# Expert up weights kept in SBUF and copied by the vector engine, in place of one load from HBM per block

## The reference, cut to what matters

```python
def _L1_ffn_ref(hidden_states, gate_w, e_bias, up_w, down_w, shared_up_w, shared_down_w):
    x = hidden_states.reshape(-1, H)                       # 2048 x 256
    topk_idx, topk_w = _router(x, gate_w, e_bias)          # 6 of 32 experts per token
    combine = jnp.zeros((T, N_EXPERTS)).at[jnp.arange(T)[:, None], topk_idx].add(topk_w)
    h = _relu2(jnp.einsum('th,eih->tei', x, up_w))         # 128 hidden units per expert
    h = h * combine[:, :, None]
    moe_out = jnp.einsum('tei,ehi->th', h, down_w)
    shared = _relu2(x @ shared_up_w.T) @ shared_down_w.T
    return (moe_out + shared).reshape(B, S, H)
```

## Time and profile before

| what | value |
|---|---|
| median of 3 runs | 829.08 us (828.86 to 834.64) |
| the profiled execution's own time | 829.08 us |
| its span | 827.3 us |
| PE busy over the span | 718.7 us (87%) |
| DVE / ACT / POOL busy | 392.1 / 276.7 / 309.9 us |
| DMA moved | 190.57 MB, mean 230 GB/s |
| mean granted TensorE clock | 0.939 of full speed |
| chain that ended last | PE 48%, POOL 17%, DVE 12%, DMA 10%, issue 9% |

### The profile page before, as it was taken

How to read it: one execution, slowest core, us unless ns; L and a number is a source line. 1 busy time by engine, 2 the same in 40 slices (tenths; PEclk the granted TensorE clock), 3 DMA queues, 4 the chain that set the end, 5 groups by cost and what they waited for, 6 DMA issues and landing times.

```text
span 827.3 us, 14657 instructions
## 1 busy us (share of the span) xinstructions
PE 718.7 (87%) x4703; PEld 633.6 (77%) x4703; DVE 392.1 (47%) x1508; ACT 276.7 (33%) x625; POOL 309.9 (37%) x328
## 2 busy tenths in 40 slices
PE   3898999989999999999999975898782799968766
PEld 3777788989999999999989953666561799957654
DVE  5999875223223223233223358788610344436453
ACT  2644532211111111111111123443330477745540
POOL 1333413730111011011010100777777277777670
PEclk9998877999999999999999986999996799989997
DMA  8999998358676676677673233555343899999996
GB/s 255 397 276 226 226 225 218 110 185 284 212 242 215 209 242 214 209 236 224 210 225 117 83 124 96 192 166 164 132 166 119 264 356 349 351 337 395 398 313 252
DMA packets 109945, 190.57 MB, mean 230 GB/s; under 512 B 11681, under 2 KB 75766, under 8 KB 109726
## 3 DMA queue, kind: packets, MB, share of 16 engines
q1 hardware_dynamic: 94464, 148.05, 58.4%
q0 software_dynamic: 13344, 38.68, 12.3%
q10 hardware_dynamic: 2046, 2.71, 1.1%
HBM read 143.44 MB, written 65.62 MB: 253 GB/s over the span
## 4 chain that ended last, share of the span: by engine, by line
PE 48%; POOL 17%; DVE 12%; DMA 10%; issue 9%; SPq 3%; ACT 1%; POOLq 0%; DVEq 0%; ACTq 0%
PE PB L598 21%; PE PB L623 12%; POOL rows_in L1880 11%; DMA MEM<-in_w 4%; POOL sorted_x L1846 4%; PE PB L814 3%; PE PB L825 3%; POOL rows_out L1892 2%; DMA X<-in_x 2%; PE PB L800 1%; PE PB L526 1%; DMA MEM<-rows_out 1%; DVE WK L1279 1%; DMA rows_out<-WS,MEM 1%; SPq L2093 1%
## 5 line engine op out<-in xcount | busy, mean ns | idle before, releaser
L598 PE MATMUL PB<-XT,MEM 128*128 128x128 f32 x1584 | 183.0, 275 | 0.6 <-DMA MEM<-in_w 0.4
L598 PEld LDWEIGHTS PB<-XT,MEM 128*128 128x128 f32 x1584 | 179.7, 192 | 1.1 <-DMA MEM<-in_w 0.6
L1855 POOL DMA_INDIRECT sorted_y<-WK x36 | 34.6, 962 | 260.1 <-DVE WK L1466 260.1
L1880 POOL DMA_INDIRECT rows_in<-MEM x96 | 94.0, 979 | 77.4 <-DVE MEM L1664 48.7
L623 PE MATMUL PB<-MEM,WK 128*128 x432 | 99.2, 379 | 0.0
L623 PEld LDWEIGHTS PB<-MEM,WK 128*128 128x128 f32 x432 | 79.3, 190 | 9.3
L814 PE MATMUL PB<-MEM 128*128 128x128 f32 x456 | 63.4, 284 | 17.6 <-DMA MEM<-in_w 17.6
L932 ACT ACTIVATE XT<-PB 128x256 f32<-128x256 f32 x52 | 20.0, 384 | 168.8 <-PE PB L580 168.8
L814 PEld LDWEIGHTS PB<-MEM 128*128 128x128 f32 x456 | 57.6, 198 | 20.2 <-issue 10.8
L1892 POOL DMA_INDIRECT rows_out<-WS,MEM x58 | 57.5, 992 | 33.6 <-ACT WS L1071 17.5
L1443 DVE TENSOR_TENSOR WK<-WK,PB 64x128 f32<-64x128 f32 x36 | 10.5, 292 | 114.4 <-ACT WK L942 114.4
(11 more groups left out here) (259 smaller groups left out, 1204.3 us busy)
## 6 DMA issues: line engine op xcount, KB each, us to landing
MEM<-in_w SPq DMA_DIRECT2D x36, 896.0 KB, 7.1
rows_in<-in_consts SPq DMA_DIRECT2D x32, 600.0 KB, 14.1
MEM<-in_w SPq DMA_DIRECT2D x148, 128.0 KB, 2.3
MEM<-in_w SPq DMA_DIRECT2D x36, 512.0 KB, 4.1
MEM<-rows_in SPq DMA_DIRECT2D x58, 300.0 KB, 4.9
MEM<-rows_out SPq DMA_DIRECT2D x16, 768.0 KB, 7.2
MEM<-in_w SPq DMA_DIRECT2D x2, 3072.0 KB, 19.4
sorted_x<-MEM SPq DMA_DIRECT2D x1, 5070.0 KB, 39.4
```

The source lines that it names most:

```text
L598: t = e.matmul(o[:, to:to + P], UPW[m][i % (3 - m)][:, k, c * P:(c + 1) * P], XT[:, n % 2, k, :], start=(k == 0), stop=(k == 1))
L1855: e.indirect_dma_start(out=DY, out_offset=bass.IndirectOffsetOnAxis(ap=DEST[:, i:i + 1], axis=0), in_=YS[:, i % 2, :], in_offset=None).the ...
L1880: e.indirect_dma_start(out=DX1, out_offset=bass.IndirectOffsetOnAxis(ap=SLOT1[:, i, j:j + 1], axis=0), in_=XR[:, i, :], in_offset=None).th ...
```

## The change

SP no longer loads up weights in the last stage. `load_expert` now loads both halves of an expert (256 KB instead of 128 KB, 32 times), so that `W1E` holds up and down weights of all experts. DVE reads the table of experts and copies the up weights of each block, 128 x 256 numbers, from `W1E` to a small buffer `WUP` (two pairs deep), at an address that comes from a register. PE's `up2` waits for that copy ("bw"). DVE makes the copies of pair s+1 right behind the multiplication of pair s, ahead of `sum_rows`; the reading of the table and `meta1` stand ahead of the multiplication.

```diff
-        W1E = MEM[:, 0:E1 * 256].rearrange("p (e c) -> p e c", e=E1)
-        W1U = MEM[:, 9216:11264].rearrange("p (a b c) -> p a b c", a=4, b=2)
+        W1E = MEM[:, 0:E1 * 512].rearrange("p (e c) -> p e c", e=E1)
+        WUP = WK[:, 3116:4140].rearrange("p (a b c) -> p a b c", a=2, b=2)
...
             def up2(s):
                 q.wait_ge("bxt", s)
-                q.wait_ge(f"wu{s % 4}", s)
+                q.wait_ge("bw", s)
...
-                        t = e.matmul(PB[:, 4 + s % 4, j * P:(j + 1) * P], W1U[:, s % 4, j, k * P:(k + 1) * P],
+                        t = e.matmul(PB[:, 4 + s % 4, j * P:(j + 1) * P], WUP[:, s % 2, j, k * P:(k + 1) * P],
                                      XTB[:, s % 3, j, k, :], start=(k == 0), stop=(k == 1))
...
+            def weights2(s):
+                q.wait_ge("bu", s - 2)
+                for j in range(2):
+                    t = e.tensor_copy(WUP[:, s % 2, j, :], W1E[:, bass.ds(expert(packed, 2 * s + j), 1), 0:256].rearrange(
+                        "p e c -> p (e c)"))
+                t.then_inc(*q.mark("bw", s))
+
...
             def step(s, n_pairs):
                 if s + 1 < n_pairs and (s + 1) % 2 == 0:
+                    q.wait_ge("tabe")
+                    if s < 0:
+                        for j in range(4):
+                            q.wait_ge(f"w1{j}", 8 * j + 7)
+                    packed[(s + 1) // 2] = four_experts(q, (s + 1) // 2)
+                    if s < 0:
+                        weights2(0)
                     meta1((s + 1) // 2)
                 if 0 <= s < n_pairs:
                     ht = HT1[:, s % 3, :, :].rearrange("p b c -> p (b c)")
                     q.wait_ge("brl", s)
                     e.tensor_tensor(ht, ht, PB[:, 4 + s % 4, 0:256], ALU.mult).then_inc(*q.mark("bh", s))
+                if 0 < s + 1 < n_pairs:
+                    weights2(s + 1)
...
-                    e.dma_start(W1E[:, k, :], w1[SC + k, :, 256:512]).then_inc(*q.land(f"w1{k // 8}", k))
+                    e.dma_start(W1E[:, k, :], w1[SC + k]).then_inc(*q.land(f"w1{k // 8}", k))
...
-            def weights2(s):
-                q.wait_ge("tabe")
-                if s // 2 not in packed:
-                    packed[s // 2] = four_experts(q, s // 2)
-                q.wait_ge("bu", s - 4)
-                for j in range(2):
-                    e.dma_start(W1U[:, s % 4, j, :],
-                                w1[bass.ds(expert(packed, 2 * s + j) + SC, 1), :, 0:256].rearrange("e p c -> p (e c)")
-                                ).then_inc(*q.land(f"wu{s % 4}", *((s,) if j else (s, "first"))))
```

More of the change, by code:

```diff
@@ L95 @@
     "cleared": ("set", "hb0"),
[L96 to L99, removed]
 }.items() for signal in list_}
@@ L823, in down2 @@
                 for j in range(2):
-                    w = W1E[:, bass.ds(expert(packed, 2 * s + j), 1), :].rearrange("p e c -> p (e c)")
+                    w = W1E[:, bass.ds(expert(packed, 2 * s + j), 1), 256:512].rearrange("p e c -> p (e c)")
                     t = e.matmul(PB[:, 2 + s % 2, j * D:(j + 1) * D], HT1[:, s % 3, j, :], w, start=True, stop=True)
@@ L1747, in dve_program @@
             number1 = e.value_load(PAGES, min_val=0, max_val=P)
+            packed = {}
             def meta1(k):
@@ L2083, in store @@
                 e.dma_start(od[:, i:i + 2, :], X[:, i:i + 2, :]).then_inc(*q.land("out_a", i))
-            packed = {}
-            def weights2(s):
-                q.wait_ge("tabe")
-                if s // 2 not in packed:
-                    packed[s // 2] = four_experts(q, s // 2)
-                q.wait_ge("bu", s - 4)
-                for j in range(2):
-                    e.dma_start(W1U[:, s % 4, j, :],
-                                w1[bass.ds(expert(packed, 2 * s + j) + SC, 1), :, 0:256].rearrange("e p c -> p (e c)")
-                                ).then_inc(*q.land(f"wu{s % 4}", *((s,) if j else (s, "first"))))
-            for s in range(3):
-                weights2(s)
             fetched = 6
@@ L2103, in step @@
             def step(s, n_pairs, fetched):
-                if 3 <= s + 3 < n_pairs:
-                    weights2(s + 3)
                 for k in range(fetched, min(s + 8, n_pairs + n_pairs % 2)):
@@ L2121, in end1 @@
                 n_pairs, k = PAIRS[c], fetched
-                packed.clear()
                 for s in range(COMMON, n_pairs + 2):
```

## The result

| | before | changed |
|---|---|---|
| median of 19 runs each | 834.64 us | 841.01 us |
| lowest and highest | 828.86, 838.26 us | 837.46, 846.13 us |
| profiled execution, span | 829.08, 827.3 us | 839.12, 837.3 us |

The ratio is 1.0077, with a 95% interval of 1.0056 to 1.0097: the changed kernel is slower by about 6.4 us. The forecast was 838.5 us, and the range (825 to 862) holds the time. The profiled execution of before was at the low end of its 19 runs, so the two profiles are 10.0 us apart, the two medians 6.4 us.

The account below looks back on a forecast made before the run. POOL was taken to bound the last stage, with 7 us to spare. Last up2 12.7 us later, tail 3.8 us shorter, larger loads 0.5 us: 9.4 us on the profiled 829.08, so 838.5 us, range 825 to 862.

Parts of the forecast that it names:

- the ring: Last stage: up2, relu, square, two copies, next up2 wait on each other in turn; 2.72 us a pair, against POOL's 2.54.
- Part 1: Last stage: 114 loads of 128 KB go, and PE's 17.6 us of waits; gains at most POOL's spare 7 us.
- Part 2: Between the layers: 32 loads grow by 128 KB each, 4.2 MB in all; costs 0.5 us.
- Part 3: Last stage's new loop: up2 waits for copies behind the previous square, so the bound leaves POOL; 2.72 us a pair.
- DVE to PE: In the last stage's loop, the hand-off from DVE's finished copies to PE's next up2: 0.01 us.
- register instructions in the open: Three register instructions ahead of each DVE copy run mostly hidden; 0.05 us a pair, 0.68 if fully exposed.
- meetings with POOL: In the last stage DVE's copies are sometimes slowed by POOL's scatters: 0.06 us a copy, 0.12 a pair.
- Part 4: Last stage: sum_rows between copies and next square is no longer free where meta1 also runs; 8.0 us in sum.
- The tail: From last up2 to the end of the last scatter: about 6.5 us instead of 10.3, 3.8 us less.
- Rival (b): Last stage: the loop hides behind POOL's scatters, so the stage stays POOL's; 822 us, or 825 with some sum_rows; chance 0.22.
- Rival (a): DVE's register instructions ahead of the copies stay exposed, 0.68 us a pair: 871 us, half exposed 854; chance 0.25.
- rival (c): Last stage: DVE's copies and POOL's scatters shut each other out, 0.37 us a copy, 35 us in all: 873 us; chance 0.08.

Follow-up runs that it names:

- ahead_again: The changed kernel with copies made two pairs ahead and WUP four pairs deep, on the 834 us chip: 828.95 us, ratio 0.9935 to the kernel before.
- sums_again: The changed kernel with the sums of steps 38, 44 and 50 moved one step later, on the 834 us chip: 837.37 us, ratio 1.0029 to the kernel before.
- changed_again: The changed kernel, unaltered, measured once more against the kernel before on the 834 us chip: 840.84 us, ratio 1.0096.
- PE's read: The changed kernel with PE's table read ahead of up2 in even steps: 976.31 us, ratio 1.0088 to the kernel before; on the 834 us chip 840.70 us, 1.0076.

## Why the prediction was right, and where its terms were off

**The bound before (POOL)** holds: with the ring open and every copy still there, POOL's "issue" row is back at 105 scatters, and the stage takes 148.4 us from first to last scatter. That wins 3.4 us of the 7 to spare in the traces; the medians differ by 5.0 us.

**Part 1, the loads that go**: right that they are worth at most POOL's spare 7 us. In ahead_again, which has this gain and no ring, it is 5.0 us by the medians and 0.0065 x 834 = 5.4 us by the ratio, other small costs already taken off.

**Part 2, the larger loads**: forecast 0.5 us; the direct tests give 0 within 3 us, the first up2 comes 3.1 us later between the two profiles, and the comparison of the stages leaves -0.7 to +2.4 us. Not settled within that.

**Part 3, the ring**: the mechanism is right, and ahead_again shows it. Its size is not: forecast 2.72 us, measured 2.56, or 2.60 as a mean of undisturbed steps, some of which end with PE's own table read and not with the copies.

| term | forecast | measured |
|---|---|---|
| up2 to relu | 1.20 | 1.20 |
| relu to square | 0.42 | 0.42 |
| square to copies | 0.34 | 0.34 |
| two copies | 0.50 | 0.49 |
| DVE to PE | 0.01 | 0.11 |
| register instructions in the open | 0.05 | 0 |
| meetings with POOL | 0.12 | 0 |
| the row chosen high for overlaps | 0.08 | 0 |

The forecast took 2.55, the middle of 2.47 to 2.63, before it added registers and meetings (0.08 in the last line). The largest miss on the other side is DVE to PE: rows 7 has a matmul behind DVE, here it is a weight load, 0.11 us behind the copies. The register instructions are in the trace and cost DVE next to nothing: ahead of all 114 copies it was idle for 2.5 us in 3 places. The view of one line's instructions, for the copies of the changed kernel (count, ns min/median/max, first and last start):

```profile
L1769 DVEq ALU_OP  x199: 40/45/64, 609.4 to 804.5; - x199
L1769 DVEq FUSED_REGOPS  x114: 57/57/71, 609.5 to 804.6; - x114
L1769 DVE COPY WK<-MEM x114: 273/288/506, 609.6 to 805.0; 128x256 f32 x114
```

45 and 57 ns each, where the forecast carried over SP's 0.34 us for three. The median copy is 288 ns as worked out from the earlier trace rows, and the mean 298, so meetings with POOL cost 0.01 us a copy, not 0.06. They do occur: of the 114 copies 7 took over 0.35 us. All 7 began 0.55 to 0.70 us after the start of a scatter, and all ended 1.05 us after that start, as the second copy here:

```profile
779.41 0.96 POOL L1905 DMA_INDIRECT rows_out<-MEM  x1 [0.30 <-issue]
779.75 0.71 DVE L1769 COPY WK<-MEM 128x256 f32 x2
```

In ahead_again it is 20 copies, begun 0.53 to 0.68 us into a scatter, with the same 1.05 us (1.06 in a few) to their end; the mean copy there is 319 ns. Copies that began in other parts of a scatter took at most 0.35 us. So a copy is held up by a part of a scatter, for up to 0.24 us, and not by the whole.

The table read of DVE also was cheaper than forecast: 0.44 us idle ahead of `meta1` at 690.79 us, not 0.6, and the square behind it still had to wait 0.20 us for the relu, where the forecast left 0.14.

**Part 4, sum_rows**: right in kind and nearly in size. The steps of up2 behind 38 and 40, 44 and 46, 50 and 52, and 54 took 3.34, 3.30, 3.71, 3.35, 3.54, 3.00 and 4.60 us, in sum 24.84 - 7 x 2.57 = 6.9 us over the ring, against 8.0. sums_again takes 3.5 us (medians) to 5.6 us (ratios) away by moving the first six of these, 4.7 us between first and last up2 (forecast for those: 5.9). What the forecast lacked is other steps over 2.57 us: 154.5 - 56 x 2.57 - 6.9 = 3.7 us, from PE's table read, the first step (3.30 us), and a few steps whose cause is open.

**The tail**: forecast 6.5 us, measured 9.3. It counted two scatters behind the last up2. There are four: the pair before waits too, since its down2 stands in PE's queue behind that up2.

**The sum**: 9.4 us forecast; 10.0 us between the profiles, 6.4 us between the medians. That the total came out so close to 10.0 is partly luck: the ring (56 x 0.15 = 8.4 us) and sum_rows (1.1) were too long, and the other steps (3.7), the tail (2.8), the start (2.6) and the end of the span (1.0) that much too short. That 838.5 lies so close to 841.01 is luck again: the base, 829.08, was 5.6 us below the median of 19 runs, and the increase 3.0 us above the measured one. The forecast gave 0.59 to "slower by over 1%"; it came out as slower by 0.8%, and 1.0% in changed_again.

**Rival (b)** gave 2.6 us as the length from which it decides, and the ring is below it; yet the stage isn't POOL's alone. The step that fails in it is its "with some of the 8 us of sum_rows left, 825". At 2.57 against POOL's 2.54 the ring hides nothing: POOL has no backlog from which to cover a long step, so each of them is paid. Its price of 822 to 825 us, set against the same low profile, is what a kernel gets that really hides the copies (0.9935 x 829.08 = 823.7). **Rival (a)** falls with 45 ns register instructions, **rival (c)** with the 0.99 us scatter and the copies of 298 and 319 ns on average, in two kernels. By the rule of the Trainium skill ("SBUF — State Buffer", Who interferes with whom) the one that comes first, a float32 copy in SBUF or a GpSimd instruction, holds the shared ports for its whole length and blocks the other. The traces bear out the blocking, but not the whole length: the longest copy of the changed kernel took 0.51 us, where waiting out a scatter could add up to 0.96 us, and most copies begun inside a scatter lost nothing. The other way round it is small too: the 33 scatters that began while a copy ran and met no addition took 1.01 us on average, the 67 others 0.96 us.

## What to carry to other kernels

Before moving a producer onto an engine that also consumes, walk once round: if the new work sits behind something that depends on the step it feeds, the engines stop overlapping, and the length of that ring, not the busy time of any engine, is the step. The same copies cost 0.8 to 1.0% or gain 0.65%, depending on being issued one or two pairs ahead. And compare the ring with the old bound only together with everything else in that queue: a ring that is as long as the bound has no slack to hide the occasional long instruction.

## What the runs showed that I had not expected

- Address registers on DVE are nearly free: 45 and 57 ns an instruction, hidden behind the instruction before; on SP three took 0.34 us.
- Two float32 copies of 128 x 256 in SBUF take 0.49 us together. Copy and scatter meet only in a part of the scatter: a copy that begins 0.55 to 0.70 us into one ends 1.05 us after the scatter's start, up to 0.22 us late in the changed kernel. The mean scatter hardly changed (0.992 and 0.996 us, 0.987 and 0.992 before). The wide additions lengthen one more: the earlier trace rows.
- A weight load that waits for DVE's copies is shown as waiting for "issue", 0.33 us. The end of the copies in the timeline (0.11 us earlier) is what tells.
- The same kernel takes 834 us on one chip and 968 us on two others. From 560 to 740 us one of these had PE busy 92.5 of 180 us with a granted clock of 0.72, where its first profile had 142.3 us at 0.90. The opened kernel's gain is half as large there (0.9968 against 0.9935), while the ratios of the moved sums (1.0032 and 1.0029) and of PE's read (1.0088 and 1.0076) are alike on both. Why these chips are slower stays open.
